# Six local-attention layers: another order of units in a two-round schedule, on all engines

## The reference, cut to what matters

```python
def attn_layer(x, Wqkv, qs, ksc, Wo):
    q, k, v = heads(x @ Wqkv)                       # 16 heads of 64
    q, k = l2norm(q) * qs, l2norm(k) * ksc
    q = q * cos * scale + rotate_half(q) * sin * scale
    k = k * cos / scale + rotate_half(k) * sin / scale
    return local_attention(q, k, v) @ Wo            # windows of 32, each sees itself and the one before

def ffn_layer(x, g, bln, W1, b1, W2, b2):
    xn = (x - mean) / sqrt(var + 1e-05) * g + bln
    a, gate = split(xn @ W1 + b1)
    return a * gelu(gate) @ W2 + b2

for i in range(6):
    x = attn_layer(shift_tokens(x), ...) + x
    x = ffn_layer(shift_tokens(x), ...) + x
```

## Time and profile before

| | us |
|---|---|
| median of 3 runs | 4416.38 (4402.02 to 4422.89) |
| the profiled execution, own time | 4408.29 |
| its span | 4406.5 |
| PE busy | 3530.6 (80%) |
| DVE busy | 2674.6 (61%) |
| ACT busy | 1983.6 (45%) |
| POOL busy | 1217.7 (28%) |

### The profile page before, as it was taken

One profiled execution on the slowest core, in us unless ns is written; L12 is line 12 of the kernel. 1 busy time (PEld: TensorE's weight loads), 2 busy tenths in 40 slices (PEclk: granted clock), 3 DMA queues, 4 the chain that ended last, 5 costly groups with the idle time before them and its releaser, 6 DMA issues. The chain is left out here.

```text
span 4406.5 us, 96135 instructions
## 1 busy us (share of the span) xinstructions
PE 3530.6 (80%) x40572; PEld 2371.0 (54%) x40572; DVE 2674.6 (61%) x4567; ACT 1983.6 (45%) x3505; POOL 1217.7 (28%) x813
## 2 busy tenths in 40 slices
PE   7565779999999957998395588888888885699996
PEld 4445546777777746332123345555555554466774
DVE  4124565666666653887757566767766664566663
ACT  1032335555555523887202245455544542335552
POOL 1002105555555423000002354444444430200000
PEclk9576889999999978999697799999999997889997
DMA  1023200000000035000001100000000000100000
GB/s 37 5 63 106 81 35 1 9 1 9 1 1 1 1 93 194 2 1 1 4 1 56 62 2 22 23 8 22 12 22 7 2 2 16 30 17 18 9 3 10
DMA packets 73830, 109.24 MB, mean 25 GB/s; under 512 B 14434, under 2 KB 56090, under 8 KB 72636
## 3 DMA queue, kind: packets, MB, share of 16 engines
q1 hardware_dynamic: 70396, 96.86, 7.3%
q0 software_dynamic: 3008, 6.23, 0.4%
HBM read 86.37 MB, written 10.94 MB: 22 GB/s over the span
## 5 line engine op out<-in xcount | busy, mean ns | idle before, releaser
L1990 PE MATMUL narrow_ps_t<-narrow_Q,narrow_KQ 32*128 32x256 f32 (+2 forms) x2176 | 386.2, 402 | 6.6 <-DVE narrow_maskedT L2142 3.1
L3521 POOL TENSOR_TENSOR local_turn<-local_turn 128x1024 f32<-128x1024 f32 x96 | 226.8, 2362 | 515.9 <-DVE local_turn L3579 515.8
L2076 ACT ACTIVATE narrow_probsT<-narrow_ps_t 128x512 f32<-128x512 f32 (+1 forms) x448 | 232.9, 566 | 223.2 <-PE narrow_ps_t L1990 220.7
L2549 POOL TENSOR_TENSOR wide_probs<-wide_probs,wide_factor 128x1024 f32<-128x1024 f32 x128 | 239.6, 1893 | 311.5 <-ACT wide_factor L2510 311.5
L2506 ACT ACTIVATE wide_probs<-wide_ps_s,wide_nm 128x1024 f32<-128x1024 f32 (+1 forms) x256 | 237.2, 927 | 173.3 <-DVE wide_nm L2591 153.2
L2953 PE MATMUL bonds_ps<-bonds_act_of,bonds_out 128*32 128x448 f32 (+3 forms) x1024 | 281.0, 566 | 24.8 <-ACT bonds_rows L2936 18.6
L2126 DVE TENSOR_REDUCE narrow_part<-narrow_ps_s 128x1 f32<-128x512 f32 x384 | 236.2, 683 | 104.7 <-PE narrow_ps_s L1973 104.7
L1990 PEld LDWEIGHTS narrow_ps_t<-narrow_Q,narrow_KQ 32*128 32x128 f32 (+1 forms) x2176 | 274.7, 186 | 45.6 <-ACT narrow_probsT L2076 21.5
L1973 PE MATMUL narrow_ps_s<-narrow_KQ 32*128 32x512 f32 x768 | 255.2, 674 | 34.4 <-DMA narrow_KQ<-narrow_close 17.3
L2586 DVE TENSOR_REDUCE wide_nm<-wide_ps_s 128x1 f32<-128x1024 f32 x128 | 156.0, 1219 | 195.2 <-PE wide_ps_s L2392 195.2
L2902 DVE TENSOR_TENSOR bonds_strain<-peri_in_moved 128x1664 f32<-128x1664 f32 (+3 forms) x128 | 257.4, 2088 | 4.4 <-ACT bonds_act_of L2925 3.6
(11 more groups left out here) (594 smaller groups left out, 8159.3 us busy)
## 6 DMA issues: line engine op xcount, KB each, us to landing
moe_w<-in_L_ffn_w SPq DMA_DIRECT2D x62, 512.0 KB, 4.9
local_wqkv<-in_L_ffn_qkv SPq DMA_DIRECT2D x6, 1536.0 KB, 6.7
context_rows<-in_ctx SPq DMA_DIRECT2D x8, 768.0 KB
context_keys<-in_ctx_T SPq DMA_DIRECT2D x6, 800.5 KB, 4.5
narrow_KQ<-narrow_close SPq DMA_DIRECT2D x64, 58.0 KB
wide_source<-in_ctx_T SPq DMA_DIRECT2D x4, 800.5 KB, 4.2
narrow_source<-in_ctx_T SPq DMA_DIRECT2D x4, 800.5 KB, 4.8
local_wo<-in_L_ffn_out SPq DMA_DIRECT2D x6, 512.0 KB, 4.8
```

Of the source, the lines that this page charges most:

```text
L1990: mm = pe.matmul(bank[0:hi - lo, at:at + q1 - q0], KQ_of(s)[part_of(h), lo:hi], Q2[part_of(h), s % RING, q0:q1], start=True, stop=True, sk ...
L2076: act.activation(probsT[0:high, c % PROBS, h, 0:wide], bank[0:high, 0:wide], ACT.Exp).then_inc(t_taken_act.sem, 1)
L2549: pool.tensor_tensor(v, v, factor[:, n // 4 % 2, j:j + 1].broadcast_to([P, CUT]), ALU.mult).then_inc(lowered[i].sem, 1)
L3521: pool.tensor_tensor(turn1[:, n % 2, j, :, :], turn1[:, n % 2, j, :, :], turn2[:, j, :, :], ALU.add)
```

## The change

`rounds()` is written anew, with an own order for odd and even rounds. In the terms of the plan:

- `exp` stands ahead of `va`, so on ACT the exponentials come ahead of the copy of V's first half.
- `k` stands ahead of `pt` (and in even rounds ahead of `ga`).
- `ga` and `gb` stand one behind the other.
- `vb` stands ahead of `s`; before it was behind it.
- `gd` and `xs` move: `gd` of a group was in an even round behind `vb`, and is now in the odd round that follows, behind `pt`. `xs` was at the front of that odd round and now stands behind `ot`.
- `gv` moves from behind `k` to behind `vb`, `gx` (DVE's normalising, L3623 and L3625) from behind `s` to the end of the round.
- The sum of squares (L3582, L3584) is an entry of its own, `sum`, behind `qt`; before it stood in DVE's part of `k`.
- The table for Exp and Ln is loaded explicitly in `root` of the even rounds in which a `ga` exists, no longer behind `gb`. The last such round is 46, while `ga` goes on in rounds 48, 50 and 52.

In the order lists a row is a run of equal instructions; local_ps are the PSUM slots.

```diff
-        for r in range(ROUNDS + 6):
-            yield from [("q", r), ("xs", (r - 7) // 2 if r % 2 else -1), ("kt", r - 1), ("va", r), ("gm", (r - 5) // 2 if r % 2 else -1),
-                        ("exp", r - 2), ("pt", r - 2), ("ga", (r - 6) // 2 if r % 2 == 0 else -1), ("k", r),
-                        ("gb", (r - 6) // 2 if r % 2 == 0 else -1), ("gv", (r - 5) // 2 if r % 2 else -1), ("qt", r - 1), ("ot", r - 3),
-                        ("root", r), ("s", r - 1), ("gx", (r - 5) // 2 if r % 2 else -1), ("rest", r), ("vb", r),
-                        ("gd", (r - 6) // 2 if r % 2 == 0 else -1), ("wo", r - 3), ("o", r - 2), ("sh", (r - 4) // 2 if r % 2 == 0 else -1)]
+        for r in range(ROUNDS + 7):
+            yield from [("q", r), ("kt", r - 1), ("exp", r - 2), ("va", r)]
+            if r % 2:
+                shift, last = (r - 5) // 2, (r - 7) // 2
+                yield from [("gm", shift), ("k", r), ("pt", r - 2), ("gd", last), ("qt", r - 1), ("sum", r), ("ot", r - 3), ("xs", last),
+                            ("root", r), ("vb", r), ("gv", shift), ("s", r - 1), ("rest", r), ("wo", r - 3), ("o", r - 2), ("gx", shift)]
+            else:
+                g = (r - 6) // 2
+                yield from [("k", r), ("pt", r - 2), ("ga", g), ("gb", g), ("qt", r - 1), ("sum", r), ("ot", r - 3), ("root", r), ("vb", r),
+                            ("s", r - 1), ("rest", r), ("wo", r - 3), ("o", r - 2), ("sh", (r - 4) // 2)]
...
                 elif kind == "root":
+                    if ("ga", (n - 6) // 2) in rank and n % 2 == 0:
+                        act.preload_act_table_set("natural_log_exp_and_others")
...
-                    if kind == "gb":
-                        act.preload_act_table_set("natural_log_exp_and_others")
...
-                    if j:
-                        for side in range(2):
-                            dve.tensor_reduce(ss[:, n % 2, side, :], sq[:, side, :, :], AX.X, ALU.add)
-                        dve.drain()
-                        dve.tensor_scalar(ss[:, n % 2, :, :], ss[:, n % 2, :, :], 1e-24, None, ALU.max).then_inc(ss_ready.sem, 1)
+                elif kind == "sum":
+                    for side in range(2):
+                        dve.tensor_reduce(ss[:, n % 2, side, :], sq[:, side, :, :], AX.X, ALU.add)
+                    dve.drain()
+                    dve.tensor_scalar(ss[:, n % 2, :, :], ss[:, n % 2, :, :], 1e-24, None, ALU.max).then_inc(ss_ready.sem, 1)
```

## The result

| | us |
|---|---|
| before, median (4 runs) | 4419.64 (4402.02 to 4431.37) |
| changed, median (4 runs) | 4290.04 (4268.25 to 4297.76) |
| ratio | 0.9684, 95% interval 0.9657 to 0.9711 |
| the profiled execution of the changed kernel | 4292.73, its span 4290.9 |
| the local layers, from their first matmul to the first of the next stage, before | 1138.8 (2515.6 to 3654.4) |

The forecast was 4282 us, from a sum of -134. The stage itself became 142.1 us shorter. All that lies outside it took 26 us more in this execution (4290.9 - 996.7 = 3294.2, before 4406.5 - 1138.8 = 3267.7) although it is the same program; a second profile of the changed kernel had 3279.0. The 26 us lie in PE's own work: outside the stage it was busy for 2631 us at a granted clock of 0.87 and 0.85 (ahead of the stage and behind it), before for 2600 at 0.87 and 0.87.

A forecast was written before the change was run, and what follows sets the result against it. PE sets the local layers' pace, with five waits adding 7.8 us a pair. Terms -114, -14, -8 and +2 gave -134: 4274 us profiled, 4282 as median after 8.1 us; 8-in-10 range 4252 to 4342.

The forecast's parts named there:

- 18 pairs: Local layers' pairs of rounds, 2743.66 to 3582.24: 724.3 us in place of 838.6, -114.
- rounds 7 to 10: Local layers, rounds 7 to 10: 80.2 us in place of 94.4, -14.
- rounds 0 to 6: Local layers' first rounds, partly without the feed-forward, fewer units between k and its slot's successor: -8 (0 to -12).
- round 47 and end: Last stretch of the local layers, 72.2 us, ruled by the latency of a single group: +2.
- The pair: An odd and an even round of the local layers: 38.6 us, 5.9 less; bounds 37.6 and 40.5.
- The service time of a slot: From the start of k to the unit that could take its slot: 5.61 us; it sets the waits that stay.
- waits and handovers: PE's idle time in a pair: 1.4 us of waits in place of 7.8, plus 0.2 for handovers not seen.
- the exponentials' move and `k`'s: exp ahead of va, k ahead of pt: PE's waits at pt (1.44 and 2.07) both go, 3.51 us a pair.
- what costs nothing: Later xs copy, gx, root, V's second copy and gd's end cost nothing as long as DVE keeps up.
- The slower rival: DVE and POOL exclude each other: DVE busy 43.8, a pair 46.8 us, +53, 4469 us; chance 0.06.
- Starving: Rival: PE gets instruction gaps in s and o every round; 32 more gaps cost 58 us, 4340; chance 0.12.
- The clock: Granted clock below 1.00 in the 18 pairs cost 16 us; half kept (ends 0 and 16).

The follow-up runs named there:

- the two kernels above: The kernel before with one change each: exp ahead of va (4397.7 us, ratio 0.9943), or k ahead of pt (4397.71 us, ratio 0.9943).
- both undone together: The changed kernel with exp behind va and pt ahead of k again: 4373.57 us, ratio 0.9879 to the kernel before, stage 1089.7.

## Why the prediction was right

**The sum.** Its terms beside what the two profiles show:

| | forecast | measured |
|---|---|---|
| 18 pairs | -114 (724.3) | -113.2 (725.4) |
| rounds 7 to 10 | -14 | -11.3 |
| rounds 0 to 6 | -8 (0 to -12) | -14.4 |
| round 47 and end | +2 | -3.2 |
| stage | -134 | -142.1 |

**The pair.** Forecast 38.6, measured 38.69 undisturbed. The waits left in the 18 pairs are 17.3 + 6.6 = 23.9 us, 1.33 in a pair, forecast 1.4. One by one: `ot` 0.69 (0.71), `qt` 0.26 to 0.36 (0.37), `k` 0.37 in the mean and up to 0.9 (0.25), `vb` none (0.1). The service time of a slot, 5.61 us, read from one place of the trace, with the units in between read from others, gave the new waits to within some 0.1 us. In part two small errors cancelled in it. From the start of `k` to the unit that took its slot it is now 5.72 us in the odd round (3344.73 to 3350.45) and 5.81 in the even one (3324.03 to 3329.84), and PE's work in between is 5.03 and 5.45, not 4.90 and 5.24: both terms came out 0.1 to 0.2 longer.

The pair as a whole is closer than its parts, too. The prediction kept PE's work at 36.96 ("the same matmuls") and added 1.6 of waits and handovers. In the undisturbed pair PE's work is 37.44 and the idle time 1.25. `k`, for one, takes 1.82 us from its start to that of the next unit, before 1.71. So PE's work with the same matmuls did depend on the order, by 0.5 us a pair; why was not looked into. That 38.6 met 38.69 to 0.1 is partly luck.

**The part that was right in sum but not in its division.** The prediction gave the exponentials' move and `k`'s 3.5 us a pair together, said "1.5 + 1.7 is more than either", and did not ask what covers the chain behind. By itself the first brings 0.6%, since `gv` then waits for POOL and PE's work behind that wait runs at a lower clock; the prediction did not price the move of `gv` at all, nor that of `xs`, which it filed under what costs nothing. The kernel without the xs move is 37 us slower. So those two are necessary parts of the gain, and the prediction had them only because it worked through the new order as a whole. For `xs` that is measured (with `gd` in the even round); for `gv` it is argued from the waits at L3433 in the two kernels above, since no run puts `gv` alone back.

**DVE.** The forecast had it busy for 32.2 of 38.6 us, 83%. It was busy for 31.1 of 38.7, 80%, and for less than the 32.1 to 32.8 of before: the xs copy lost 2.2 us and the scaling of the normalising (L3629) 1.5, while the copy into shifted gained 1.1 and the product ahead of the scaling (L3627) 1.3. The slower rival, DVE and POOL shutting each other out, did not come true, though collisions of that kind did arise (below).

**Starving.** This rival fell: 12 gaps of 21.5 us became 18 gaps of 17.1. All but one still lie in `s` and `o`. They come more often and shorter, so the closer order did not cost more in sum.

**The clock.** The mean granted clock in the 18 pairs rose from 0.97 to 0.99, both the level of 2.4 GHz with short stretches of 1.2 GHz. I had kept half of 16 us. But the 16 rested on waits of 7.5 us in every pair, and the rows of waits above give 128.4 us, 7.1 a pair, since the gate product was waited for in 12 pairs only. PE's busy time gives the division of the 18 pairs more directly:

| 18 pairs, us | before | forecast | measured |
|---|---|---|---|
| PE's work, 18 times that of the undisturbed pair | 665.3 | 665.3 | 673.9 |
| PE's busy time beyond that | 23.2 | 8 | 9.5 |
| waits (forecast with handovers) | 128.4 | 29.5 | 23.9 |
| no instruction | 21.5 | 21.5 | 17.1 |

(The columns add up to 838.4, 724.3 and 724.4.) The second row is where the clock below 1.00 has to be; it fell by 14, not by 8. The forecast of the sum is closer than its terms: the work was put 9 us too low, waits and gaps together 10 too high. Nearly the whole gain, 104.5 of 113.2 us, is waits that are gone, and that is the mechanism that was forecast.

**Beginning and end** were mis-sized, both to the good. In rounds 0 to 6 the granted clock was 0.95 (before 0.93 from 2515.6 to 2649.2), at the end 0.98 (before 0.91). The end did get its table loads:

```profile
3513.88 1.28 ACT L3500 ACT_TABLE_LOAD   x1
...
3516.55 0.47 ACT L3500 ACTIVATE local_rstd<-local_ps,local_eps 128x256 f32<-128x256 f32 x1 [1.39 <-PE local_ps L3437]
3517.09 1.28 ACT L3502 ACT_TABLE_LOAD   x1
3518.39 0.42 ACT L3502 ACTIVATE local_rstd<-local_rstd 128x256 f32<-128x256 f32 x1
```

The load for Ln lay in ACT's waiting time; the one for Exp stood in the chain, 1.28 us, and Exp began 1.30 after it. There is no further 1.38 of drain, as the Trainium skill, "ScalarE: Activation LUTs", section "What ACT_TABLE_LOAD costs", would have it; the trace decides. I had counted two loads for Exp in the chain, 2.6 us. For the group before this one they did not count: Exp was done at 3504.09, while DVE, which needs its result, was dividing the output until 3505.3. So one of the two stood in the chain. PE's busy time in this stretch fell from 54.9 to 52.7 us at the better clock, and that outweighed it.

## What to carry to other kernels

Where several units pass through few buffers in a fixed order, measure a buffer's service time once (here 5.6 us from the start of the matmul to DVE's last read) and fill the units between a slow one and its successor in the slot until they exceed it; count to exactly that successor, for removing a unit also changes who waits. Several moves can cover one and the same latency: a single move on the old order (0.6% here) and a single one undone on the new (0.2 to 0.6%) both understate it, and only both undone together show its size (2%). And look what a wait covers before it is taken away: the next chain behind it becomes the wait, and behind one that lasted 2.49 us in one piece, in place of 1.44 and 1.50, the granted clock fell as well. Take PE's work in a pair with some reserve: it moved by 0.5 to 0.7 us between orders of the same matmuls.

## What the runs showed of the hardware

Which DVE operations are held up depends on where they fall beside POOL's, and the price moves with them. The changed kernel's 18 pairs by groups (busy us, mean ns of one | idle before):

```profile
L3627 DVE SCALAR_TENSOR_TENSOR local_centred<-local_centred,local_up,local_rstd 128x256 f32<-128x256 f32 x18 | 31.1, 1727 | 0.0
L3618 DVE COPY local_shifted<-layers_Z 64x255 f32<-64x255 f32 x18 | 24.9, 1382 | 2.0 <-issue 0.4
```

And one place from its timeline:

```profile
3320.49 1.90 POOL L3534 TENSOR_TENSOR local_turn<-local_turn,local_ss 128x1024 f32<-128x1024 f32 x1
3320.63 2.05 DVE L3627 SCALAR_TENSOR_TENSOR local_centred<-local_centred,local_up,local_rstd 128x256 f32<-128x256 f32 x1
3322.75 0.35 DVE L3629 TENSOR_SCALAR local_centred<-local_centred,local_up 128x256 f32<-128x256 f32 x1
```

The copy into shifted, 0.29 before, now takes 1.38 in the mean. The product with two inputs in SBUF began 0.14 us after POOL's and ended 0.29 after POOL was done; before, it took 0.48 in the mean. The scaling behind it is what was held up before (1.83 in the mean), and it now takes 0.35. The Trainium skill, "SBUF — State Buffer", section "Who interferes with whom", says that a DVE instruction with two SBUF inputs contends with a POOL instruction that reads SBUF; this row agrees. At the place shown neither operation is on PE's path. But the copy into shifted stands ahead of the rotation of q, whose slot `k` needs: where it took 1.71 us (from 2934.65) and a refill of the rotary table (L3550, 0.69) followed, `k` waited 0.89 in place of 0.30. In the 18 pairs `k`'s waits hold 1.2 us more than 18 times 0.30, so the price was small here.

The granted clock of PE fell behind some stretches without work and not behind others. Behind the 2.49 us at `gv` (exponentials alone moved) it was 0.63 for 3.65 us. In the kernel before it was 0.61 from 3058.59 to 3062.02, behind idle 1.20 us, work of 1.38 and idle 1.93; and it stayed at 1.00 from 3046.93 to 3055.28, behind a wait of 2.07 at `pt`.
